# Inverse softmax sums of a differential attention layer: spread over partitions by TensorE from a stationary operand of step 0 in two column tiles, in place of a ScalarE copy and two transposes

## The reference, cut to what matters

```python
s1 = einsum('bhtd,bhsd->bhts', q1, k1) * scale + mask
s2 = einsum('bhtd,bhsd->bhts', q2, k2) * scale + mask
a1, a2 = softmax(s1), softmax(s2)
diff = a1 - lam * a2
out = einsum('bhts,bhsd->bhtd', diff, v)
```

## Time and profile before

| | |
|---|---|
| runs | 1991.02 us median (1989.27 to 1998.99) |
| span of the profiled execution | 1982.6 us |
| its own time | not given apart from the three runs: the median is 8.4 us above the span |
| mean granted TensorE clock | 0.947 |
| busy, share of the span | PE 85%, PE weight loads 63%, VectorE 70%, ScalarE 59%, GpSimd 29% |
| attention stage, 60 to 1306 us | 1246 us |
| expert stage, about 1340 to 1800 us | 460 us |

### The profile page before, as it was taken

One profiled execution on the slowest core, in us unless ns is written; L12 is line 12 of the kernel. 1 busy time (PEld: TensorE's weight loads), 2 busy tenths in 40 slices (PEclk: granted clock), 3 DMA queues, 4 the chain that ended last, 5 costly groups with the idle time before them and its releaser, 6 DMA issues. The chain is left out here.

```text
span 1982.6 us, 36940 instructions
## 1 busy us (share of the span) xinstructions
PE 1681.3 (85%) x9718; PEld 1251.6 (63%) x9719; DVE 1394.1 (70%) x3225; ACT 1166.2 (59%) x3388; POOL 578.0 (29%) x471
## 2 busy tenths in 40 slices
PE   4878898898899899889889889873999999999800
PEld 3556556656566655656656665543999999999700
DVE  4998888988888988888898898744333333333377
ACT  2777878877788788787887887832222222222133
POOL 0322322522432432241251252012533342100075
PEclk8999999999999999999999999985999999999955
DMA  8764755765574574484575566014533344433187
GB/s 280 229 169 128 202 139 139 213 170 150 170 202 120 160 207 124 133 232 125 149 229 144 139 203 179 24 71 175 164 118 118 109 127 148 132 95 94 65 258 250
DMA packets 141462, 311.40 MB, mean 157 GB/s; under 512 B 16608, under 2 KB 19296, under 8 KB 140160
## 3 DMA queue, kind: packets, MB, share of 16 engines
q1 hardware_dynamic: 111264, 231.64, 41.3%
q0 software_dynamic: 15072, 50.74, 7.7%
q10 hardware_dynamic: 14976, 27.27, 3.6%
HBM read 207.87 MB, written 101.71 MB: 156 GB/s over the span
## 5 line engine op out<-in xcount | busy, mean ns | idle before, releaser
L856 ACT ACTIVATE expd<-S,neg_max 128x128 f32<-128x128 f32 (+3 forms) x1024 | 530.9, 535 | 152.5 <-DVE neg_max L1042 151.3
L1042 DVE TENSOR_REDUCE neg_max<-S 128x2 f32<-128x768 f32 (+3 forms) x384 | 399.5, 1040 | 144.9 <-PE S L664 135.7
L1073 DVE SCALAR_TENSOR_TENSOR mixed<-expd,rho 128x384 f32<-128x384 f32 (+3 forms) x512 | 338.8, 681 | 0.0
L660 PE MATMUL S<-kT,qT 128*128 128x256 f32 (+2 forms) x1024 | 276.7, 373 | 30.0 <-DMA qT<-parts_rows 18.2
L675 PE MATMUL PTp<-ident,mixed 128*128 128x128 f32 x1280 | 211.7, 280 | 57.4 <-DVE mixed L1073 53.0
L868 ACT ACTIVATE probsT<-PTp 128x512 f32<-128x512 f32 (+2 forms) x384 | 205.2, 534 | 91.3 <-PE PTp L675 88.8
L1529 ACT ACTIVATE xT_hi<-xTp 128x512 fp32r<-128x512 f32 x72 | 43.1, 599 | 357.9 <-DVE yo L1710 352.0
L660 PEld LDWEIGHTS S<-kT,qT 128*128 128x128 f32 x1024 | 162.5, 193 | 132.5 <-issue 92.0
L722 PE MATMUL tail<-wo,ctxT 128*128 128x512 f32 x464 | 218.9, 595 | 0.3
L856 ACT ACTIVATION_READ_ACCUMULATOR expd<-S,neg_max 128x1 f32 x1024 | 216.7, 212 | 0.0
L555 POOL TENSOR_TENSOR swapped<-swapped,rope_t 128x512 f32<-128x512 f32 x77 | 99.1, 1287 | 397.2 <-DVE swapped L1035 397.2
(11 more groups left out here) (245 smaller groups left out, 3632.7 us busy)
## 6 DMA issues: line engine op xcount, KB each, us to landing
qT<-parts_rows SPq DMA_DIRECT2D x256, 256.0 KB, 4.5
parts_rows<-parts SPq DMA_DIRECT2D x160, 256.0 KB, 2.8
wqk<-wqk_split SPq DMA_DIRECT2D x75, 512.0 KB, 6.1
xin<-expert_in_rows SPq DMA_DIRECT2D x72, 256.0 KB, 3.0
expert_out_rows<-yo ACTq DMA_DIRECT2D x72, 256.0 KB, 3.2
kT<-parts_rows SPq DMA_DIRECT2D x64, 256.0 KB, 4.2
x<-in_x SPq DMA_DIRECT2D x8, 1024.0 KB, 7.2
x_rows<-x SPq DMA_DIRECT2D x8, 1024.0 KB, 7.3
```

The source lines that it names most:

```text
L660: nc.tensor.matmul(S[s % 2][:, k * slot:k * slot + w], qT[kv % 2][:, 2 * h + c, i * P:(i + 1) * P], kT[kv][:, c, 0:w], start=(k % per_bank ...
L856: ex = nc.scalar.activation(expd[s % 3][:, k * slot:k * slot + w], S[s % 2][:, k * slot:k * slot + w], ACT.Exp, bias=neg_max[s % 3][:, k:k ...
L1042: nc.vector.tensor_reduce(neg_max[s % 3][:, 0:k], v, AX, ALU.max, negate=True).then_inc(max_ready, 1)
L1073: ins = nc.vector.scalar_tensor_tensor(out=mixed[sl % 3][:, a * 256:a * 256 + w], in0=e2, scalar=rr[:, i, h:h + 1], in1=e1, op0=ALU.mult, ...
```

## The change

In `values`, the two transposes of `rwide` become four products, one for each head: the stationary operand is the column of `rsum` of head h, read 64 times with step 0 (128 rows x 64 columns), the moving operand is the identity (128 columns), and the output is the half of the partitions that belongs to the head. Heads 2p and 2p+1 use the two column tiles. The product sums `rsum[k, h] * ident[k, q]` over k, which is `rsum[q, h]` in each of 64 partitions. The products read `rsum` directly, so the wait on `rwide_ready` becomes one on `rsum_step`, and `widen` with its buffers, its semaphore and its calls is gone from ScalarE.

```diff
@@ values, TensorE
-                pe.wait_ge(rwide_ready, g + 1)
+                pe.wait_ge(rsum_step, u + 1)
                 for pair in range(2):
-                    nc.tensor.transpose(O[:, 1, pair, :], rwide[i % 2][:, pair * P:(pair + 1) * P], ident[:])
+                    for half in range(2):
+                        h = 2 * pair + half
+                        nc.tensor.matmul(O[half * HD:(half + 1) * HD, 1, pair, :],
+                                         rsum[kv % 2][:, i, 0, h:h + 1].broadcast_to([P, HD]), ident[:],
+                                         start=True, stop=True, tile_position=(0, half * HD))
@@ ScalarE
-            def widen(sl, u, g):
-
-                i, kv = LAST_OF[sl % NU], sl // NU
-                act.wait_ge(rsum_step, u + 1)
-                at_least(act, ctx_full, g - 1)
-                nc.scalar.activation(rwide[i % 2][:].rearrange("p (h d) -> p h d", h=RK),
-                                     rsum[kv % 2][:, i, 0, :].unsqueeze(2).broadcast_to([P, RK, HD]),
-                                     ACT.Copy).then_inc(rwide_ready, 1)
@@ ScalarE, body
-                    if (s - 2) % NU in LAST_OF and lagged(b, s, 2, first):
-                        widen(*lagged(b, s, 2, first), tile_no(b, s, 2))
@@ ScalarE, end
-                    if s < 2 and (s - 2) % NU in LAST_OF:
-                        widen(*lagged(b, s, 2, False), tile_no(b, s, 2))
```

More of the change, by code:

```diff
@@ L220, in attention_block @@
         probsT = [sb(f"probsT{r}", [P, NT - 1 + r, 2, 2, P]) for r in range(2)]
-        rwide = [sb(f"rwide{r}", [P, RK * HD]) for r in range(2)]
         scale = sb("scale", [P, 2, P])
@@ L289, in attention_block @@
         rho_step = sem("rho_step")
-        rwide_ready = sem("rwide_ready")
         scale_out = sem("scale_out")
```

## The result

The changed kernel takes 2011.16 us, median of 4 runs (2005.79 to 2017.23), beside 1995.01 us of the kernel before in its 4 runs (1989.27 to 1999.33): ratio 1.0094, interval 1.0062 to 1.0126. So the change makes the kernel slower by 16 us by the medians and 19 by the ratio in the first series, and by 13 to 16 in the second, where +15 was forecast. The forecast time of 2006 us, in a range of 1990 to 2022, stood on a median of 1991 us for the kernel before; in this series it has 1995, and that accounts for 4 of the 5 us between 2006 and 2011.

What follows compares the result with a forecast made beforehand. No engine was near full; in the attention ring of PE, DVE and ACT, PE was late most often. +19 us (PE) - 4 (ACT) = +15 on the 1982.6 us span, plus 8.4 to the median: 2006 us, range 1990 to 2022.

Steps and rivals of the forecast that it cites:

- The price on PE: Attention, TensorE: eight records at 0.43 us replace two transposes, 0.22 us more a tile, 28 us over 128 tiles.
- C: Rival: the products on TensorE cost double, 84 us more there, +54 us in all, 2045 us; chance 0.07.
- The step of 0 at no cost: TensorE's weight loads: reading a column 64 times costs nothing, hidden under streaming; upper end 84 us.
- The share, 0.69: Attention: part of TensorE's added 28 us seen in the time, middle of 0.38 and 1, giving 19 us.
- ACT's relief, 4 us: Attention, ScalarE: removing 128 copies gains 4 us, the middle of 0 and 7; most becomes idle time.
- The bound of 7 from direct waits: Upper bound of the gain on ScalarE: 50 waits, a third just behind a copy, 0.43 us each.
- ACT's busy time: Sign in the profile after: ScalarE's busy time in attention down by 55 us.
- ACT's idle time: Sign in the profile after: ScalarE's idle time in attention up by over 60 us.
- DVE's wait for the scores: Sign in attention: VectorE's wait for TensorE's scores rises from about 124 to 135 us.
- the lower share: Attention: steps in which VectorE waited for TensorE's scores, 146 / 384 = 0.38, so 10.6 of 28 us seen.
- A: Rival: TensorE's addition lies almost hidden in its waits in attention, +3.6 us, 1995 us; chance 0.24.
- B: Rival: ScalarE was the pacemaker of attention, so removing its copy gains, -17 to -18 us, 1973 us; chance 0.09.

Runs made afterwards that it cites:

- the second: The changed kernel measured once more, unaltered, in 6 runs beside the kernel before: median 2006.7 us, ratio 1.0079.
- untiled products: Kernel before with its two transposes as ordinary products of 128 array columns from ScalarE's widened copy, no column tiles: 2015.7 us, ratio 1.0112.
- The copy kept: Kernel before with the change's four products on TensorE; ScalarE's widening copy still runs, read by nobody: 2015.5 us, ratio 1.0118.
- no spread: Kernel before without copy and per-tile transposes; the scale half of O is written once with ones: 1979.0 us, ratio 0.993.
- products twice: Changed kernel with each of the four products of a tile issued twice to the same output: 2045.7 us, ratio 1.0276.
- no copy: Kernel before without ScalarE's copy; the two transposes stay and read a buffer filled once with ones: 1993.6 us, ratio 1.0.

## Why the prediction was right

**The price on PE** held to the hundredth: 0.44 us for eight records (0.49 less the 0.05 of a first pair) where 0.43 was forecast, +0.22 us a tile, 28 us. The step from 256 to 128 moving columns by halving, the side by side of the two tiles and the gap that moves without being doubled are all in the timeline after. C's double price didn't occur.

**The step of 0 at no cost** was an assumption without a row; untiled products from a widened buffer at the same time (+22 and +20) bear it out.

**The share, 0.69**, was the middle of 0.38 and 1. The copy kept gives 20 / 28 = 0.71 at equal clock, and 23.5 / 28 = 0.84 by the ratio. That the middle came out so near is luck: nothing in the rows singled it out, and the bounds allowed +3.6 to +28 us. The share isn't a constant, either: 0.5 when PE is relieved by 28 us, 0.7 to 0.8 for the first 28 us more. For the next 55 it is 0.8 at equal clock and 0.63 to 0.71 by the medians, so a further growth with the addition isn't shown. What the profiles do show is that PE's wait for the mix shrinks as PE gets more work, 59.6 us with no spread, 51 in the kernels before and after, 42.0 with the products twice. For the no-spread kernel the assumption of a constant share failed by 6 us (-24 expected, -18 found).

**ACT's relief, 4 us**, the middle of 0 and 7, came out at 4 to 5 at equal clock; by the plain ratio it is 0 in the kernel before (-3 to +3), and 5 to 8 in the changed one. That the sum of the two terms, +15, is met is therefore shown better than either term. The bound of 7 from direct waits (50 waits, a third of them behind a copy, 0.43 us each) isn't contradicted at equal clock. The forecast that ACT's busy time falls by 55 us was wrong in size: it fell by 30, because I took the mean duration for busy time while the copy overlaps its neighbours. ACT's idle time grew by 318.5 - 266.5 = 52 us (1268 - 949.5 after), somewhat under the 60 forecast. Neither bears on the sum, as ACT's time isn't the bound.

**DVE's wait for the scores** was forecast to rise to 135 us at most and stands at 153.9 (150.3 in the second profile). The forecast let 11 of PE's added 28 us show in this wait, the lower share; the two profiles have 30 and 26 more, about all of them. This was a sign and no term of the sum, but it says that the lower share, counted from the steps in which DVE already waited, was too low for that place.

**Rivals.** A (+4), B (-18) and C (+54) lie outside the intervals of both series. PE's busy time rose by 33 us instead of 28 in the profiled execution; the second profile of the change has 1147.39 us to its end at 1323, 27 more than before. Part of the difference between the two lies in stretches at the lower clock, below.

## What to carry to other kernels

Before moving work from one engine to another, compare their idle time in the stage and ask who waits for whom: here a copy of 0.4 us on ScalarE was worth at most 0.03 to 0.06 us of the end at equal clock, and 0.22 us on TensorE was worth 0.16. A transpose of 4-byte floats is one record where a product is two, so a product with the identity costs TensorE twice the transpose that it replaces. Two column tiles side by side don't win that back: they only make up for needing twice as many products. The share of an addition that is seen should not be taken over from a relief of the same size: here it was 0.5 for taking 28 us off PE and 0.7 to 0.8 for putting 28 us on it.

## What the runs showed that was not expected

The mean granted clock differs by kernel and by execution, in programs that do nearly the same work: 0.941 for the kernel without the copy, 0.944 before, 0.947 with the products twice, and within the kernel before from 0.940 to 0.948, with the times given above. The lower of the two levels, 1.2 GHz, appears in short stretches of attention. One of them, in the busy times of two stretches of the changed kernel:

```profile
1262.00:1279.00 17.00, 13.84 (x86) 8.73 (x85) 13.98 (x40) 14.13 (x41) 0.00 (x0) 1.00 0.01 2
1279.00:1290.00 11.00, 8.51 (x44) 5.76 (x42) 3.79 (x10) 9.60 (x30) 0.00 (x0) 0.53 0.00 0
```

and PE's timeline there:

```profile
1277.89 0.74 PE L658 MATMUL S<-kT,qT 128*128 128x256 f32 x4 [2.10 <-ACT expd L858]
...
1286.68 3.45 PE L693 MATMUL O<-probsT,vals 128*64 128x256 f32 x16
```

In the 17 us before the fall PE was idle 3.2 us, among them 2.1 in one wait for ACT; in the next 11 us the granted clock is 0.53, and a tile of 16 values takes 3.45 us where it takes about 1.9 at 2.4 GHz. Many of these stretches belong to the kernel and not to the execution. Both profiles of the changed kernel have a granted clock of 0.91 in 640 to 660 us, in 960 to 980 and in 1120 to 1140, and of 0.83 in 1270 to 1300, where the profile of before has 1.00 in all four and 0.91 at places of its own, such as 680 to 700. Others come in one of the two only, such as that in 800 to 820 (0.91 against 1.00). That a kernel with more work for PE (products twice) kept the higher clock and one with less for ACT (no copy) the lower is what the means say; why the second should be so stays open, and whether a slot of PE work placed in such waits would keep the clock up wasn't tried. It is also why a figure at equal clock can't stand alone here.

A second thing bears on single profiles. After the last transposes of the experts (the last of `xTp` starts at 1858.9 us before and at 1880.6 after) the program needs another 124 us before, 125 with the change and up to 135 in other profiles, though nothing was changed there. The span of the copy kept is 33 us longer than that of before and its attention only 21. So where one profile stands against one, the end of the stage that was changed says more than the span.
